# A graph-convolution gather stage: source one-hots built by two VectorE comparisons a group, gathers that read the index table in place

## What is computed

```
h = x @ W
norm = deg_inv_sqrt[src] * deg_inv_sqrt[dst]
msgs = h[src] * norm[:, None]
out = jax.ops.segment_sum(msgs, dst, num_segments=N)
...
# later layer: for every node, the row of the LAST edge that has it as edge_index[0]
dst, src = (edge_index[0], edge_index[1])
agg = jnp.zeros_like(x).at[dst].set(x[src])
```

## Time and profile before

| | us |
|---|---|
| runs | 3186.33, 3186.75, 3189.61; median 3186.75 |
| span of the profiled execution | 3429.2 (the profile gives no other time of it) |
| the gather stage in the profiled execution | 346 to 1600, that is 1254 |
| all before it, all after it | 346 and 1829 |

### The profile page before, as it was taken

How to read it: one execution, slowest core, us unless ns; L and a number is a source line. 1 busy time by engine, 2 the same in 40 slices (tenths; PEclk the granted TensorE clock), 3 DMA queues, 4 the chain that set the end, 5 groups by cost and what they waited for, 6 DMA issues and landing times. The chain is left out here.

```text
span 3429.2 us, 61808 instructions
## 1 busy us (share of the span) xinstructions
PE 2383.0 (69%) x12969; PEld 1967.6 (57%) x12970; DVE 1627.2 (47%) x4918; ACT 1494.4 (44%) x4924; POOL 1674.7 (49%) x2221
## 2 busy tenths in 40 slices
PE   3667455555565655656968999968879999930893
PEld 2445343444443444444757888846658999930792
DVE  8996233333333333335862222267766777751113
ACT  1121566656666666655432333345553444402331
POOL 3551666666666666653765200077755555404214
PEclk9559667777777777778559999989999999965896
DMA  4002322222222222221223333222221000000223
GB/s 132 0 0 78 126 84 83 84 86 82 84 82 84 82 83 80 84 73 47 78 94 114 107 107 121 93 77 62 62 64 41 15 15 14 14 27 30 61 71 102
DMA packets 150370, 242.12 MB, mean 71 GB/s; under 512 B 29912, under 2 KB 109152, under 8 KB 150194
## 3 DMA queue, kind: packets, MB, share of 16 engines
q0 software_dynamic: 55664, 144.61, 14.5%
q1 hardware_dynamic: 78402, 77.05, 6.9%
q10 hardware_dynamic: 16256, 19.93, 1.7%
HBM read 184.52 MB, written 60.16 MB: 71 GB/s over the span
## 5 line engine op out<-in xcount | busy, mean ns | idle before, releaser
L810 POOL DMA_INDIRECT all_XN<-h_table,gcn_idx x784 | 769.5, 982 | 523.1 <-ACT gcn_idx L778 289.9
L892 PE MATMUL gcn_acc<-all_XN,gcn_hot 128*128 128x256 f32 x1568 | 573.0, 530 | 461.7 <-DVE gcn_hot L850 286.1
L892 PEld LDWEIGHTS gcn_acc<-all_XN,gcn_hot 128*128 128x128 f32 x1568 | 397.8, 266 | 550.2 <-issue 230.0
L789 ACT ACTIVATE gcn_lo_gap<-l_iota,l_src_lo 128x128 f32<-128x128 f32 x784 | 307.5, 392 | 7.4 <-issue 7.3
L1317 ACT ACTIVATE moe_hidden<-moe_hid_ps,moe_b 128x128 f32<-128x128 f32 x420 | 130.6, 364 | 300.8 <-PE moe_hid_ps L1392 287.0
L790 ACT ACTIVATE gcn_hi_gap<-l_iota,l_src_hi 128x49 f32<-128x49 f32 x784 | 253.9, 324 | 11.9 <-issue 11.6
L775 ACT COPY gcn_seen_sb<-gcn_seen 128x196 f32<-128x196 f32 x196 | 63.2, 323 | 432.3 <-remote 220.7
L834 DVE SCALAR_TENSOR_TENSOR all_X<-gcn_acc,l_dinv,all_X 128x256 f32 x196 | 94.8, 484 | 302.2 <-issue 167.1
L1392 PEld LDWEIGHTS moe_hid_ps<-moe_xst,moe_w 128*128 128x128 f32 x1680 | 204.4, 193 | 28.9 <-issue 22.1
L1392 PE MATMUL moe_hid_ps<-moe_xst,moe_w 128*128 128x128 f32 x1680 | 207.8, 277 | 18.0 <-issue 16.2
L1399 PE MATMUL moe_y_ps<-moe_w,moe_hidden 128*128 128x256 f32 x840 | 199.6, 380 | 2.0 <-ACT moe_hidden L1317 1.9
(11 more groups left out here) (323 smaller groups left out, 5409.8 us busy)
## 6 DMA issues: line engine op xcount, KB each, us to landing
moe_w<-in_e_w ACTq DMA_DIRECT2D x32, 512.0 KB
moe_xs<-slots_in SPq DMA_DIRECT2D x106, 128.0 KB
slots_out<-moe_y SPq DMA_DIRECT2D x105, 128.0 KB
all_XN<-h_table,gcn_idx POOLq DMA_INDIRECT x784
all_X<-in_x SPq DMA_DIRECT2D x7, 896.0 KB
h_table<-proj_hs SPq DMA_DIRECT2D x49, 128.0 KB, 1.7
z_table<-comb_zb SPq DMA_DIRECT2D x49, 128.0 KB, 2.6
out<-all_XT SPq DMA_DIRECT2D x49, 128.0 KB
```

Of the source, the lines that this page charges most:

```text
L789: nc.scalar.activation(lo_gap[:, c, :], self.iota[:, :], ACT.Abs, bias=self.src_lo[:, ds(GE * g + c, 1)]).then_inc(gaps_ready, 1)
L810: nc.gpsimd.indirect_dma_start(msg[b][:, c, :], None, self.h_table, bass.IndirectOffsetOnAxis(idx[b][:, c:c + 1], 0)).then_inc(msg_in[b], 16)
L892: last = nc.tensor.matmul(acc[p][:, :], hot[p][:, c, :], msg[b][:, c, :], start=(c == 0), stop=(c == GE - 1))
```

## The change

The source one-hots are made on DVE, in bf16, one comparison of 128x512 for `lo_hot` and one of 128x196 for `hi_one`; ACT keeps only the scaled copy (`spot`) and `keep_seen`. `src_lo` and `src_hi` become bf16 and are no longer negated. The tiles `idx` and their semaphore go: POOL reads the index columns in `srcI` itself, its 784 gathers are written out, and before group g it waits for `seen_ready` of PE. The scratch tile `part` in the stage before is a tile of its own.

```
                     link(nc.vector.tensor_scalar(part[:, :], self.srcI[:, :], 127, None, ALU.bitwise_and))
-                    link(nc.vector.tensor_scalar(self.src_lo[:, :], part[:, :], -1.0, None, ALU.mult))
+                    link(nc.vector.tensor_copy(self.src_lo[:, :], part[:, :]))
...
+                    def spot(g, p):
+                        after(act, hi_ready, g + 1)
+                        after(act, seen_ready, g - 1)
+                        nc.scalar.activation(hi_hot[p][:, :, :], hi_one[p][:, :, :], ACT.Copy, scale=self.spot).then_inc(spot_ready, 1)
                     def step(g, b, h):
                         p = b % 2
+                        spot(g, p)
                         if not isinstance(g, int) or g >= 2:
                             keep_seen(g - 2, p)
-                        if not isinstance(g, int) or g + 2 < G:
-                            indices(g + 2, (b + 2) % NB)
-                        for c in range(GE):
-                            nc.scalar.activation(lo_gap[:, c, :], self.iota[:, :], ACT.Abs, bias=self.src_lo[:, ds(GE * g + c, 1)]).then_inc(gaps_ready, 1)
-                            nc.scalar.activation(hi_gap[:, c, :], self.iota[:, 0:T], ACT.Abs, bias=self.src_hi[:, ds(GE * g + c, 1)]).then_inc(gaps_ready, 1)
-                        after(act, gaps_ready, 9 * g + 8)
-                        nc.scalar.activation(hi_one[:, :, :], hi_gap[:, :, :], ACT.Relu, bias=self.one, scale=-1.0).then_inc(gaps_ready, 1)
-                        after(act, seen_ready, g - 1)
-                        nc.scalar.activation(lo_hot[p][:, :, :], lo_gap[:, :, :], ACT.Relu, bias=self.one, scale=-1.0).then_inc(src_hot, 1)
-                        after(act, gaps_ready, 9 * g + 9)
-                        nc.scalar.activation(hi_hot[p][:, :, :], hi_one[:, :, :], ACT.Copy, scale=self.spot).then_inc(src_hot, 1)
-                        after(act, src_hot, 2 * g + 2)
...
-                    def gather(g, b, h):
-                        after_alone(pool, self.passed, idx_ready, g + 1)
+                    for g in range(G):
+                        b = g % NB
+                        after(pool, seen_ready, g - NB + 1)
                         for c in range(GE):
+                            n = GE * g + c
                             nc.gpsimd.indirect_dma_start(msg[b][:, c, :], None, self.h_table,
-                                                         bass.IndirectOffsetOnAxis(idx[b][:, c:c + 1], 0)).then_inc(msg_in[b], 16)
-                    steps(pool, gather)
+                                                         bass.IndirectOffsetOnAxis(self.srcI[:, n:n + 1], 0)).then_inc(msg_in[b], 16)
...
                         nc.vector.tensor_tensor(hot[p][:, :, :], ...  ALU.is_equal).then_inc(hot_ready, 1)
+                        after(dve, seen_ready, g - 1)
+                        nc.vector.tensor_tensor(lo_hot[p][:, :, :], self.src_lo[:, ds(GE * g, GE)].unsqueeze(2).broadcast_to([P, GE, P]),
+                                                self.iota_bf[:, :].unsqueeze(1).broadcast_to([P, GE, P]), ALU.is_equal).then_inc(src_hot, 1)
+                        after(dve, spot_ready, g - 1)
+                        nc.vector.tensor_tensor(hi_one[p][:, :, :], self.src_hi[:, ds(GE * g, GE)].unsqueeze(2).broadcast_to([P, GE, T]),
+                                                self.iota_bf[:, 0:T].unsqueeze(1).broadcast_to([P, GE, T]), ALU.is_equal).then_inc(hi_ready, 1)
...
                     def see(g, p):
-                        after(pe, src_hot, 2 * g + 2)
+                        after(pe, src_hot, g + 1)
+                        after(pe, spot_ready, g + 1)
```

More of the change, by code:

```diff
@@ L313, in layer0_front @@
             self.dst_rel = s.sb("dst_rel", [P, ET])
-            self.src_lo = s.sb("src_lo", [P, ET])
-            self.src_hi = s.sb("src_hi", [P, ET])
+            self.src_lo = s.sb("src_lo", [P, ET], BF16)
+            self.src_hi = s.sb("src_hi", [P, ET], BF16)
             self.touch = s.sb("touch", [1, G, 3], I32)
@@ L333, in edges_stage @@
             dst_i = s.sb("dst_i", [P, ET], I32)
-            part = self.src_hi[:, :].bitcast(I32)
+            part = s.sb("part", [P, ET], I32)
             dst_lo = s.sb("dst_lo", [P, ET], BF16)
@@ L514, in _ @@
                     link(nc.vector.tensor_scalar(part[:, :], self.srcI[:, :], 127, None, ALU.bitwise_and))
-                    link(nc.vector.tensor_scalar(self.src_lo[:, :], part[:, :], -1.0, None, ALU.mult))
+                    link(nc.vector.tensor_copy(self.src_lo[:, :], part[:, :]))
                     link(nc.vector.tensor_scalar(part[:, :], self.srcI[:, :], 7, None, ALU.logical_shift_right))
-                    link(nc.vector.tensor_scalar(self.src_hi[:, :], part[:, :], -1.0, None, ALU.mult))
+                    link(nc.vector.tensor_copy(self.src_hi[:, :], part[:, :]))
                     link(nc.vector.tensor_copy(self.dstF[:, :], dst_i[:, :]))
@@ L709, in gather_stage @@
             msg = [self.XN[:, ROWS + i * GE * D:ROWS + (i + 1) * GE * D].rearrange("p (c d) -> p c d", d=D) for i in range(NB)]
-            idx = [s.sb(f"idx{i}", [P, GE], I32) for i in range(NB)]
             hot = [s.sb(f"hot{i}", [P, GE, P]) for i in range(2)]
@@ L714, in gather_stage @@
             hi_hot = [s.sb(f"hi_hot{i}", [P, GE, T], BF16) for i in range(2)]
-            lo_gap = s.sb("lo_gap", [P, GE, P])
-            hi_gap = s.sb("hi_gap", [P, GE, T])
-            hi_one = s.sb("hi_one", [P, GE, T])
+            hi_one = [s.sb(f"hi_one{i}", [P, GE, T], BF16) for i in range(2)]
             seen_sb = [s.sb(f"seen_sb{i}", [P, GE * T], I32) for i in range(2)]
@@ L726, in gather_stage @@
             iota_in = s.sem("iota_in")
-            idx_ready = s.sem("idx_ready")
             msg_in = s.sems("msg_in", NB)
@@ L730, in gather_stage @@
             src_hot = s.sem("src_hot")
+            hi_ready = s.sem("hi_ready")
+            spot_ready = s.sem("spot_ready")
             first_summed = s.sem("first_summed")
@@ L737, in gather_stage @@
             seen_copied = s.sem("seen_copied")
-            gaps_ready = s.sem("gaps_ready")
             lasts_kept = s.sem("lasts_kept")
@@ L775, in keep_seen @@
                         nc.scalar.copy(seen_sb[p][:, :].bitcast(F32), seen[p][:, :]).then_inc(seen_copied, 1)
-                    def indices(g, b):
-                        nc.scalar.copy(idx[b][:, :], self.srcI[:, ds(GE * g, GE)]).then_inc(idx_ready, 1)
+                    def spot(g, p):
+                        after(act, hi_ready, g + 1)
+                        after(act, seen_ready, g - 1)
+                        nc.scalar.activation(hi_hot[p][:, :, :], hi_one[p][:, :, :], ACT.Copy, scale=self.spot).then_inc(spot_ready, 1)
                     def step(g, b, h):
                         p = b % 2
+                        spot(g, p)
                         if not isinstance(g, int) or g >= 2:
                             keep_seen(g - 2, p)
-                        if not isinstance(g, int) or g + 2 < G:
-                            indices(g + 2, (b + 2) % NB)
-                        for c in range(GE):
-                            nc.scalar.activation(lo_gap[:, c, :], self.iota[:, :], ACT.Abs, bias=self.src_lo[:, ds(GE * g + c, 1)]).then_inc(gaps_ready, 1)
-                            nc.scalar.activation(hi_gap[:, c, :], self.iota[:, 0:T], ACT.Abs, bias=self.src_hi[:, ds(GE * g + c, 1)]).then_inc(gaps_ready, 1)
-                        after(act, gaps_ready, 9 * g + 8)
-                        nc.scalar.activation(hi_one[:, :, :], hi_gap[:, :, :], ACT.Relu, bias=self.one, scale=-1.0).then_inc(gaps_ready, 1)
-                        after(act, seen_ready, g - 1)
-                        nc.scalar.activation(lo_hot[p][:, :, :], lo_gap[:, :, :], ACT.Relu, bias=self.one, scale=-1.0).then_inc(src_hot, 1)
-                        after(act, gaps_ready, 9 * g + 9)
-                        nc.scalar.activation(hi_hot[p][:, :, :], hi_one[:, :, :], ACT.Copy, scale=self.spot).then_inc(src_hot, 1)
-                        after(act, src_hot, 2 * g + 2)
-                    for g in range(2):
-                        indices(g, g)
                     steps(act, step)
```

## The result

The changed kernel takes 3215.42 us (median of four runs, 3213.73 to 3217.02); the kernel before took 3187.63 beside it. The ratio is 1.0092, with an interval of 1.008 to 1.0104: slower by 0.9%, some 28 us. The forecast was 3209, slower. The span of the profiled execution is 3215.2 us, equal to the timed ones, so the trace of after can be laid beside the clock directly; that of before, 3429.2, can't.

What follows compares the result with a forecast made beforehand. POOL's gathers, 1.25 us apart, were taken to bound the gather stage. From 3186.75 us, -6 for the index reading, +28 for comparisons holding gathers and 0 for DVE's order gave 3209 us, range 3145 to 3256.

Steps and rivals of the forecast that it cites:

- POOL paces the stage in timed runs: Gather stage: POOL's gathers, starting 1.25 us apart, set the pace in timed runs, with 0 to 37 us of stops left.
- The sum of 1020 us: Gather stage without stops: 980 us of gather pitch, 27 of longer gathers and 13 from last gather to end.
- late signals: PE's `see` reaching ACT 5 us late in the profile; taken as mostly absent from timed runs, 242 us shorter.
- the forecast of 3401: Whole changed kernel against the profiled span: 3429.2 with 104 stops, -52 + 24 = -28, about 3401 us.
- the stops are real: Rival: POOL's 104 waits for ACT's index copy occur in timed runs too; 3159 us, down to 3117; chance 0.27.
- POOL reads the index columns itself: POOL's gathers wait for PE, not ACT's copy: 0.5 us less a stop, 1 us before the first gather; -6 us.
- The hold by the comparisons: Gathers starting inside DVE's `lo_hot` or `hi_one` wait for its end: +28 us, bounds 0, 51 and 107.
- random phase: Forecast case: comparisons meet POOL's gathers at random times, costing 0.142 us a group; 3195 to 3238 us, chance 0.42.
- one block: Rival: `lo_hot` and `hi_one` hold POOL as one operation, 51 us, and DVE late in rest groups; 3256 us, chance 0.10.
- The price of one meeting: A gather starting inside a DVE comparison with two inputs loses what is left of it less 0.12 us.
- the check by size: Hold rule for `hot` and `rest_hot` at random times gives 31 us; the trace's 27 was taken as agreeing in size.
- DVE's longer pass: DVE's queue: 1.0 us more a group, exposed only in 48 groups with a rest; 0 to 48 us, taken as 0.

Runs made afterwards that it cites:

- POOL's half: Kernel before with only index columns read in place by POOL, gathers written out and POOL released by PE's `see`; one-hots stay on ACT: 3182.89 us against 3186.20.
- the kernel with three gathers: Changed kernel with three gathers a group instead of four, the fourth column left on stale rows: 3202.72 us, ratio 0.9293 to the kernel before.
- the ramp in PSUM: Kernel before with the 128 numbers that `hot` is compared with copied into PSUM: 3170.54 us; changed kernel with all three comparisons against them: 3183.85 us.
- the wrong order: Changed kernel with ACT's index copy and POOL's loop put back, the copy behind `spot` and `keep_seen`: 3270.88 us; with the copies ahead of `spot`: 3216.31 us.
- the third comparison's run: Changed kernel with one more 128x512 bf16 comparison a group behind `lo_hot`, both inputs in SBUF, written to a spare tile: 3402.40 us, ratio 0.9876.

## Why the prediction was right

**POOL paces the stage in timed runs: right, and shown.** The sum of 1020 us for the stage without the late signals meets 1017 in the kernel that has only POOL's half, where 3.0 us of waiting are left. With ACT's one-hots in place POOL waited those 3.0 us at most, so taking 642 us of work from ACT could gain nothing, as forecast (ten of its instructions a group went besides the index copy, not twelve).

**The late signals aren't in the runs of record: right for them, though the reason was too narrow.** The prediction took them for a thing of the profiled execution. The set with the kernel before at 3445.57 us has them in its timed runs too. They come with a set of runs, perhaps with its chip (the three sets ran on three chips, and one shows them), and not with the profiling. That is why the forecast of 3401 for the profiled span was off: the trace of after was taken without them. The 0.27 for *the stops are real* was a chance that the condition holds in the runs of record, and in that set it came true in kind. What delays the signals stays open. The mean granted clock of TensorE is lower there too, 0.80 to 0.82 for the kernel before, where it is 0.85 to 0.87 in the other two sets; it isn't fixed in the late set either, since the kernel with three gathers has 0.85 to 0.86 there. Whether the lower clock is a part of the cause or comes with PE's waiting wasn't tested.

**POOL reads the index columns itself: -6 forecast, -3.3 measured.** Of the 8 us from stops there was less to get; the prediction's own two terms, 8 us and 1 us more, make 9, and it gave no reason for taking 6. One of its readings was wrong as well: it kept the 0.8 us from the copy's end to the gather as POOL's reaction to any signal. In the trace of before the median over the 104 stops is 0.80 us, but in that of after all ten stops end 0.27 us after `see` does. The waiting instructions and the sender changed together, so which of them takes the 0.53 us isn't shown. With few stops this is worth little; where there are a hundred, it is another 0.5 us a stop beside the one that was forecast.

**The hold by the comparisons: +28 forecast; the whole cost of the one-hots was about 35.** The stage of after is 35.3 us longer than that of the kernel with POOL's half alone (1052.2 against 1016.9): 24.9 us of long gathers, 8.1 of stops, 2.3 of tail. The first is the term of the prediction, in total. It isn't made as the prediction made it, though. Counted over the gathers that begin while a given DVE instruction is under way, with more than 0.12 us of it left (up to 1 us of a total is missing, where one instruction follows another):

```
                     before, profiled       only POOL's half       after
hot                  50 gathers, 14.1 us    72 gathers, 20.3 us    98 gathers, 27.0 us
lo_hot               -                      -                      71 gathers, 14.2 us
hi_one               -                      -                      34 gathers,  1.7 us
rest_hot             23 gathers,  5.1 us    14 gathers,  1.8 us    26 gathers,  3.9 us
copy to last_tile    66 gathers,  6.9 us    42 gathers,  2.5 us    31 gathers,  1.9 us
```

`lo_hot` and `hi_one` themselves cost 15.9 us, not 28: at a random phase some 88 gathers would be met with more than 0.12 us of a `lo_hot` left (196 x 0.56/1.25), and 71 were, later in it than at random (0.20 us lost a meeting, not 0.28). Another 6.7 us came from `hot`, which more gathers met than before. So that the total came out near 28 is in part luck. A random phase was a fair middle and no law; why the meetings shifted from the one to the other was not settled. Had POOL been held for both as one block, the term would have been 51; the row at 1009.84 excludes it.

**The price of one meeting: right.** The rule, what is left of the comparison less 0.12 us, gives 0.30 for the gather at 1009.84, and 0.30 was lost. Over the 67 gathers that `lo_hot` held, the loss is what was left less 0.127 us, with a standard deviation of 0.003. The durations were right too: 0.665 and 0.36 forecast, 0.686 and 0.355 measured:

```profile
L838 DVE TENSOR_TENSOR gcn_lo_hot<-l_src_lo,l_iota_bf x196: 676/684/737, 346.5 to 1392.2; 128x512 bf16<-128x512 bf16 x196
```

```profile
L841 DVE TENSOR_TENSOR gcn_hi_one<-l_src_hi,l_iota_bf x196: 347/355/420, 347.1 to 1392.9; 128x196 bf16<-128x196 bf16 x196
```

The twice faster tier of the Trainium skill (VectorE: DVE Perf Modes, "The perf-mode tier table") would have made `lo_hot` an estimated 0.42 us; by this row it doesn't apply to this operand. On the hold, the Trainium skill (SBUF — State Buffer, "SBUF: two separate sides") is borne out by the ramp in PSUM: one SBUF input instead of two, the same length, and the meetings cost at most 3 ns each.

**What else holds a gather: two of the prediction's readings were wrong.** It took the gather at 801.35 for one beside a predicated copy that isn't held up, and the rule for narrower than it is written. That gather begins 0.39 us before the copy at 801.74, so it says nothing. Where a gather begins inside the copy, the same trace shows the hold:

```profile
692.07 0.38 DVE L826 COPY_PREDICATED gcn_last_tile<-gcn_seen_sb,gcn_tile_no 128x196 f32<-128x196 int32 x1
692.17 1.07 POOL L810 DMA_INDIRECT all_XN<-h_table,gcn_idx  x1 [0.30 <-issue]
```

The copy of L825 has the same shape, but one of its inputs, `seen`, lies in PSUM, and it holds nothing (13 gathers in the trace of before, 24 in that of after, no loss in either):

```profile
1583.12 0.37 DVE L825 COPY_PREDICATED gcn_last_seen<-gcn_seen_sb,gcn_seen 128x196 f32<-128x196 int32 x1 [0.28 <-DVE all_X L843]
...
1583.24 0.94 POOL L810 DMA_INDIRECT all_XN<-h_table,gcn_idx  x1 [0.30 <-issue]
```

This also takes away the check by size: of the 27 us of long gathers before, `hot` and `rest_hot` make 19.2, where the rule at a random phase gave 31, and the copy that was left out makes 6.9. That 31 stood near 27 was luck. The second reading is that of the earlier trace rows: inside the loop POOL's additions don't take 1614 ns, they take 0.73 or 1.8 to 2.3 us, mostly in turn. The 1614 is a mean of these, and the row doesn't show what a comparison costs. That bf16 comparisons hold POOL is shown by `lo_hot` in the table above.

**DVE's longer pass: taken as 0, it cost about 10 us. This is the step that was mis-sized.** All of after's ten stops lie between 1293 and 1375, near the end of the stage, where groups often reach into a further tile: from 1190 on a rest comes every 10 to 16 us, that is in about every second group. But the 100 us before 1290 have nine rests and no stop and the 100 after it eight, so density alone isn't it; that POOL's lead has to be used up first fits, and isn't shown. One of the stops, on the kernel after's timeline:

```profile
1334.23 0.69 DVE L835 TENSOR_TENSOR gcn_hot<-l_dst_rel,l_iota 128x512 f32<-128x512 f32 x1
1334.83 0.69 DVE L838 TENSOR_TENSOR gcn_lo_hot<-l_src_lo,l_iota_bf 128x512 bf16<-128x512 bf16 x1
...
1335.43 0.36 DVE L841 TENSOR_TENSOR gcn_hi_one<-l_src_hi,l_iota_bf 128x196 bf16<-128x196 bf16 x1
1335.70 0.48 DVE L819 SCALAR_TENSOR_TENSOR all_X<-gcn_acc,l_dinv,all_X 128x256 f32 x1
...
1337.59 0.67 DVE L835 TENSOR_TENSOR gcn_hot<-l_dst_rel,l_iota 128x512 f32<-128x512 f32 x1
...
1338.32 3.78 PE L883 MATMUL gcn_acc<-all_XN,gcn_hot 128*128 128x256 f32 x8 [0.74 <-DVE gcn_hot L835]
...
1340.87 0.69 DVE L825 TENSOR_TENSOR gcn_rest_hot<-l_dstF,all_XN 128x512 f32 x1 [0.83 <-issue]
...
1341.89 2.54 PE L874 MATMUL gcn_rest_acc<-all_XN,gcn_rest_hot 128*128 128x256 f32 x8
...
1344.27 0.26 PE L894 MATMUL gcn_seen<-gcn_hi_hot,gcn_lo_hot 128*128 128x49 bf16 x4
...
1344.80 0.95 POOL L797 DMA_INDIRECT all_XN<-h_table,l_srcI  x1 [1.96 <-PE gcn_seen L894]
```

Read it from below: POOL waits 1.96 us for `see`; `see` comes behind the rest's product, that behind the product at 1338.32, which PE starts when `hot` is done; and `hot` stands in DVE's queue 3.36 us behind the `hot` before, of which `lo_hot` and `hi_one` fill 0.87 us (1334.83 to the start of `add_up` at 1335.70). The prediction named this chain and its bounds, 0 to 48 us, and chose its lower end because POOL was groups ahead. It isn't ahead there. The pass of DVE isn't alone in this: the product at 1338.32 took 3.78 us, where the quicker one of the earlier trace rows took 1.97, and the granted clock is 0.82 from 1330 to 1340 and 0.67 in the ten us after. But the kernel with POOL's half alone has such products in its last groups too (3.5 us at 1316.16, 1326.49 and 1336.65) and not one stop, so the difference between the two is DVE's pass. In the kernels with the ramp in PSUM, where no gather is held up and POOL is earlier, the same pass costs 15.8 us of stops and 5.3 of tail.

**The sum.** -3.3 + 24.9 + 8.1 + 2.3 is 32, and 28 to 31 us were measured; -6 + 28 + 0 was forecast as 22. The sign and the mechanism were right. Of the 10 us between 22 and 32, the pass of DVE is 10 and the smaller gain of the index reading 3, and the hold was 3 smaller than forecast.

## What to carry to other kernels

Where one engine's instructions follow each other at a fixed pitch that alone fills a stage, taking work off other engines gains nothing, and what has to be priced is what the new work does to that engine: here a VectorE operation with two SBUF inputs beside GpSimd's indirect DMAs cost each gather that met it what was left of it less 0.12 us, and moving one small operand to PSUM took that away without making the operation longer. A copy that releases a buffer belongs ahead of whatever in its queue waits for later work: the wrong order cost 55 us here. And where a profiled execution is 7.6% longer than the timed ones, the waits that it alone shows are a condition that other runs may have, not a constant part of the kernel.

## What the runs showed of the hardware that was not expected

- A comparison of 128x512 with its ramp in PSUM is as fast as with both inputs in SBUF (0.680 us against 0.682), and gathers beside it last at most 3 ns longer instead of 200 to 280. bf16 and float32 comparisons hold POOL alike, and so does a predicated copy with two SBUF inputs (0.10 us in the mean of 66 gathers of before).
- Two comparisons back to back don't act as one: the gather gets in between them (56 of 57 in the kernel after, as at 1009.84).
- PE's signals reached POOL and ACT late ("remote", 70.9 us in 37 waits of the third comparison's run) through a whole set of timed runs: the kernel before took 3443 to 3456 us there, and 3180 to 3192 in the others. Within a set the runs of a kernel agree within about 0.4%, so one can't tell from a single set which condition it is in.
